# Expert stages: all 40 row gathers issued ahead of the first scatter

## The chip, the core and the metric

One core of a Trainium2 chip runs the whole program. The metric is the device time of one execution in microseconds (us), as the median over runs.

## What is computed

The reference is a stack of six blocks on an input of 8 x 512 tokens of 128 values. The change touches the two "L1" feed-forward blocks (called the expert stages here), of which the reference computes:

```python
logits = xf @ router_w.T
probs = jax.nn.softmax(logits, axis=-1)
topw, topi = jax.lax.top_k(probs, K)                   # K = 2 of E = 8 experts
topw = topw / (topw.sum(-1, keepdims=True) + 1e-06)
order = jnp.lexsort((-fw, fe))                         # by expert, heaviest first
keep = rank < capacity                                 # 1.25 * 4096 / 8 = 640 slots an expert
disp = jnp.zeros((E, capacity + 1, D), x.dtype).at[se, pos].set(xf[st])
g = jnp.einsum('ecd,edf->ecf', disp, wg)
u = jnp.einsum('ecd,edf->ecf', disp, wu)
eo = jnp.einsum('ecf,efd->ecd', jax.nn.silu(g) * u, wd)
contrib = gathered * (sw * keep.astype(x.dtype))[:, None]
out = jnp.zeros_like(xf).at[st].add(contrib)

x = x + 0.5 * _L0_ffn_ref(_layernorm(x, axis=-1), ...)
x = x + _L0_attn_ref(_layernorm(x, axis=-1), ...)
x = x + 0.5 * _L0_ffn_ref(_layernorm(x, axis=-1), ...)
x = x + 0.5 * _L1_ffn_ref(_layernorm(x, axis=-1), ...)  # expert stage s = 0
x = x + _L1_attn_ref(_layernorm(x, axis=-1), ...)
x = x + 0.5 * _L1_ffn_ref(_layernorm(x, axis=-1), ...)  # expert stage s = 1
```

## The kernel before

The program is written out without loops at run time. Each engine has its own instruction stream; they meet at semaphores. The work of most blocks is ordered by a table of due times (`program_order`), but an expert stage stands by itself: the function `experts1(s)` of each engine, for s = 0 (between the second L0 feed-forward block and the L1 attention) and for s = 1 (the end of the program).

An expert stage first searches, for every expert, the weight above which its 640 tokens lie, and writes a table `token_of` of 40 columns: column r = 5 e + t holds the 128 token numbers of tile t of expert e (`SLOT_TILES` = 5, `SLOT_ROWS` = 40). VectorE writes it at L1955. From then on it goes by expert, e = 0 to 7:

- POOL (`gather_rows`, L2066 to L2079) issues one indirect DMA for each column (L2076), which fetches 128 rows of 136 values from the tensor `tokens` in HBM into `rows_in[e]`. Each of the 8 experts has its own `rows_in`: six lie in the memory of a stack buffer, the last two in the arena.
- TensorE turns the gathered tiles (`turn_gathered`, L828), ScalarE and VectorE split them into two halves (L1427, L1969), after which 16 products of three matmuls each follow (L823: eight "gate" and eight "wide" results in five PSUM banks taken in turn). ScalarE applies Silu to a gate result (L1473), VectorE multiplies it with the wide result (L1992). TensorE turns the next expert's tiles and then multiplies with the down weights ("narrow", L1159, 40 matmuls in two parts), and ScalarE scales the result by the slot's weight into `rows_out[e % 2]` (L1486). Before that it waits for the scatters of expert e - 2, which read the same buffer.
- POOL (`scatter_rows`, L2081 to L2091) issues five indirect DMAs (L2088) that add the rows to `sums` (s = 0) or to the output (s = 1) in HBM. Since two experts can write the same token, the first scatter of expert e waits until all of expert e - 1 have landed.
- SyncE loads the weights, 256 KB each (`load`, L2111): gate and up weights of expert e + 3 when those of expert e + 1 have been split, down weights of expert e + 2 when expert e is done.

How far the gathers run ahead is set by two numbers, AHEAD (experts gathered before the first scatter) and BETWEEN (gathers issued ahead of each later expert's scatters), in POOL's `experts1`:

```python
                gathered = AHEAD * SLOT_TILES
                gather_rows(range(gathered))
                for e in range(EXPERTS):
                    if e:
                        more = min(gathered + BETWEEN, SLOT_ROWS)
                        gather_rows(range(gathered, more))
                        gathered = more
                    scatter_rows(e)
```

After stage 0, SyncE waits for the last scatter and loads X back from `sums` (L2111), with which the L1 attention begins. After stage 1 it waits for the last scatter and the program ends.

Of the kernel before, what the change touches and what calls it, by code (L numbers as in the profile page):

```python
# [61 lines left out]
HALF = P // 2  # L62
PER_ROW = P // EXPERTS
REACHED = 4.0
AHEAD, BETWEEN = 4, 4
NARROW = ((0, 2), (2, SLOT_TILES))


# [2245 lines left out]
```

## Time and profile before

| | |
|---|---|
| median of 3 runs | 2848.12 us (2844.03 to 2848.57) |
| profiled execution: its own time | 2866.33 us |
| profiled execution: span | 2864.2 us |
| TensorE busy | 2597.2 us (91%) |
| VectorE busy | 2070.6 us (72%) |
| ScalarE busy | 1913.6 us (67%) |
| POOL busy | 1673.6 us (58%) |
| mean granted TensorE clock | 0.955 |
| indirect DMAs issued by POOL | 80 gathers (L2076), 80 scatters (L2088) |

Busy time is what the engine spent in instructions; for an indirect DMA on POOL that is the time in which POOL makes the DMA's descriptors, not the transfer. The shares are means over the whole program; the expert stages take some 200 us at two places, about 1570 to 1780 us and 2655 to 2864 us. In a timeline the bracket behind an instruction says how long its engine had stood idle before it, and what ended that. "issue" is time in which nothing that the profile shows was waited for.

### The profile page before, as it was taken

How to read it: one execution, taken by the hardware profiler on the slowest of the kernel's cores; microseconds unless marked ns; L12 is line 12 of the kernel's file. 1: busy time of each engine (PE TensorE's matmuls, PEld its weight loads, DVE VectorE, ACT ScalarE, POOL GpSimd, SP SyncE). 2: the span in 40 equal slices, each digit the busy share in tenths (PEclk: the TensorE clock that was granted, in tenths of full speed). 3: DMA queues.
4: the chain of work that ended last, by engine and by line, in shares of the span. 5: the costliest groups of instructions: out<-in, count | busy, mean ns of one | idle time of the engine just before them, and what ended most of it. 6: DMA issues, size and time to landing. Idle time of an engine off the chain costs nothing. (4 is left out here: it accounts for less than half of the span.)

```text
span 2864.2 us, 51642 instructions
## 1 busy us (share of the span) xinstructions
PE 2597.2 (91%) x18932; PEld 1774.7 (62%) x18932; DVE 2070.6 (72%) x4694; ACT 1913.6 (67%) x4049; POOL 1673.6 (58%) x836
## 2 busy tenths in 40 slices
PE   7999999999999999998998286999999999998286
PEld 6996555555555565646887176565665666665176
DVE  5677888888888889885776633778778778776632
ACT  5665777687777777776775143878778778776143
POOL 0002989898989889893110176656556556555077
PEclk9999999999999999998999598999999999999588
DMA  3014554454544454540001244000000000000133
GB/s 107 1 60 111 120 122 120 114 139 112 133 113 120 119 130 113 122 101 16 20 17 27 69 89 67 1 2 9 9 2 9 9 2 9 9 2 9 40 80 51
DMA packets 144649, 179.21 MB, mean 63 GB/s; under 512 B 30547, under 2 KB 74128, under 8 KB 143888
## 3 DMA queue, kind: packets, MB, share of 16 engines
q1 hardware_dynamic: 130320, 165.20, 22.8%
q0 software_dynamic: 14080, 10.73, 2.8%
q8 instruction: 152, 2.49, 0.4%
q14 instruction: 97, 0.79, 0.1%
HBM read 56.51 MB, written 17.72 MB: 26 GB/s over the span
## 5 line engine op out<-in xcount | busy, mean ns | idle before, releaser
L2047 POOL TENSOR_TENSOR arena<-arena 128x2048 f32<-128x2048 f32 x192 | 882.0, 4595 | 216.9 <-ACT arena L1353 200.3
L1658 DVE TENSOR_REDUCE top<-psum 128x1 f32<-128x512 f32 x1024 | 649.4, 683 | 79.5 <-PE psum L937 79.4
L937 PE MATMUL psum<-stack 98*128 98x512 f32 (+1 forms) x2048 | 604.8, 423 | 15.6 <-ACT arena L1353 9.3
L1353 ACT ACTIVATE arena<-psum 128x512 f32<-128x512 f32 x1024 | 546.6, 599 | 48.1 <-PE psum L937 47.7
L1008 PE MATMUL psum<-arena,values 128*32 128x512 f32 (+1 forms) x3072 | 484.5, 603 | 3.5 <-ACT arena L1353 2.6
L937 PEld LDWEIGHTS psum<-stack 98*128 98x128 f32 (+1 forms) x2048 | 357.1, 191 | 210.3 <-DVE top L1658 87.5
L2057 POOL TENSOR_TENSOR by_query<-by_query,row_tables 128x1024 f32<-128x1024 f32 x170 | 321.7, 1900 | 217.1 <-DVE row_tables L1664 215.9
L1656 DVE TENSOR_REDUCE row_tables<-psum 128x1 f32<-128x512 f32 x512 | 335.6, 679 | 2.7 <-PE psum L945 1.7
L1008 PEld LDWEIGHTS psum<-arena,values 128*32 128x32 f32 (+1 forms) x3072 | 128.6, 119 | 276.7 <-issue 252.2
L1676 DVE COPY arena<-psum 128x512 f32<-128x512 f32 x256 | 175.7, 689 | 120.4 <-PE psum L989 119.4
L2017 POOL TENSOR_SCALAR rstd<-mv 128x4 f32<-128x4 f32 x56 | 13.2, 235 | 415.6 <-DVE mv L1522 413.2
L1369 ACT ACTIVATE by_query<-psum,row_tables 128x512 f32<-128x512 f32 x340 | 231.6, 690 | 12.2 <-DVE row_tables L1656 8.9
L2057 POOL TENSOR_TENSOR arena<-arena,row_tables 128x1024 f32<-128x1024 f32 x86 | 162.8, 1899 | 118.9 <-DVE row_tables L1664 118.2
L1401 ACT ACTIVATE arena<-psum 128x512 f32<-128x512 f32 x128 | 76.9, 601 | 205.2 <-PE psum L1008 205.2
L823 PE MATMUL psum<-stack 128*128 128x512 f32 x768 | 212.9, 414 | 0.6 <-DVE X L1612 0.5
L1612 DVE SCALAR_TENSOR_TENSOR X<-psum,weight,X 128x128 f32<-128x128 f32 x512 | 144.0, 344 | 83.9 <-PE psum L889 83.1
L1382 ACT ACTIVATE arena<-psum 128x512 f32<-128x512 f32 x256 | 153.6, 603 | 63.1 <-PE psum L989 61.4
L1273 ACT ACTIVATE arena<-arena 128x512 f32<-128x512 f32 x256 | 158.6, 629 | 54.0 <-DVE arena L1603 44.3
L889 PEld LDWEIGHTS psum<-arena 128*128 128x128 f32 x1536 | 184.9, 192 | 7.0 <-ACT arena L1273 0.4
L889 PE MATMUL psum<-arena 128*128 128x128 f32 x1536 | 186.6, 275 | 0.0
L823 PEld LDWEIGHTS psum<-stack 128*128 128x128 f32 x768 | 138.5, 193 | 24.9 <-DVE X L1612 0.9
L1992 DVE TENSOR_TENSOR arena<-psum,arena 128x320 f32<-128x320 f32 x128 | 60.7, 490 | 128.1 <-ACT arena L1473 64.4
(208 smaller groups left out, 4685.1 us busy)
## 6 DMA issues: line engine op xcount, KB each, us to landing
stack<-halves SPq DMA_DIRECT2D x768, 128.0 KB, 2.4
qk_ring<-qk_split SPq DMA_DIRECT2D x64, 256.0 KB, 2.9
v_ring<-v_split SPq DMA_DIRECT2D x32, 256.0 KB, 3.0
tokens<-xn SPq DMA_DIRECT2D x16, 256.0 KB, 2.4
arena<-in_wg SPq DMA_DIRECT2D x16, 256.0 KB
arena<-in_wu SPq DMA_DIRECT2D x16, 256.0 KB
arena<-in_wd SPq DMA_DIRECT2D x16, 256.0 KB
wqkv<-in_w_qkv SPq DMA_DIRECT2D x2, 1536.0 KB, 9.1
```

What stands on the lines that cost most here:

```text
L823: ins = T_.matmul(out_ap, weights[w], moving[m], start=i == 0, stop=i == 2)
L889: ins = T_.matmul(bk[:, t * P:(t + 1) * P], h[:, c, t * P:(t + 1) * P], w[:, c, :], start=c == 0, stop=c == 1)
L937: return T_.matmul(bk, st[0:k, side, h, cols], st[0:k, 1 - side, h, :], start=True, stop=True)
L1008: ins = T_.matmul(bk[c, :], values[:, n % N_VALUES, kt, c], by_key[n % 2][:, kt, h, :] if l else prob[(n * TILES_B + kt) % N_PROB][:, h, : ...
L1273: S_.activation(part, part, ACT.Square).then_inc(squared, 1)
L1353: S_.activation(prob[tile % N_PROB][:, h, :], psum[:, bank[key], :], ACT.Exp, scale=scale).then_inc(released[bank[key]], 1)
L1369: S_.activation(by_query[i // HEADS[1] % len(by_query)][:, h, :], psum[:, bank[key], :], ACT.Exp, bias=peak[n % 2][:, qt, h:h + 1], accum_ ...
L1656: V_.reduce_max(peak[i][:, qt, h:h + 1], psum[:, bank[key], :], AX.X, negate=True).then_inc(peaked, 1)
L1658: give(V_.reduce_max(top[i][:, j:j + 1], psum[:, bank[key], :], AX.X), key)
L1676: give(V_.tensor_copy(by_key[n % 2][:, :, :, j * HALF:(j + 1) * HALF], psum[:, bank[key], :].rearrange("p (t h q) -> p t h q", t=TILES_B, ...
L2047: G_.tensor_tensor(to, old, prob[tile % N_PROB], ALU.add).then_inc(summed, 1)
L2057: G_.tensor_tensor(rows[:, :, :], rows[:, :, :], row_share[n % 2][:, qt, :].unsqueeze(2).to_broadcast([P, HEADS[1], SEQ]), ALU.mult).then_ ...
```

## The change

AHEAD becomes 8, so that `gathered` is 40 before the loop and `gather_rows` gets an empty range each time within it.

```diff
-AHEAD, BETWEEN = 4, 4
+AHEAD, BETWEEN = 8, 4
```

On POOL, stage 0 (`tokens` gathered to `rows_in` and, for experts 6 and 7, to the arena; `sums<-arena` are the scatters):

```order
 L2076 DMA rows_in_71<-tokens,arena 128x136 x5
 L2076 DMA rows_in_72<-tokens,arena 128x136 x5
-L2088 DMA sums<-arena 4736x128 x5
-L2076 DMA rows_in_73<-tokens,arena 128x136 x4
-L2088 DMA sums<-arena 4736x128 x5
-L2076 DMA rows_in_73<-tokens,arena 128x136
-L2076 DMA rows_in_74<-tokens,arena 128x136 x3
-L2088 DMA sums<-arena 4736x128 x5
-L2076 DMA rows_in_74<-tokens,arena 128x136 x2
-L2076 DMA arena<-tokens,arena 128x136 x2
```

The 20 gathers of experts 4 to 7 stood in groups of four behind the scatters of experts 0 to 4.

```order
+L2076 DMA rows_in_73<-tokens,arena 128x136 x5
+L2076 DMA rows_in_74<-tokens,arena 128x136 x5
+L2076 DMA arena<-tokens,arena 128x136 x10
+L2088 DMA sums<-arena 4736x128 x40
```

Now the 40 gathers stand in one row, and the 40 scatters behind them in another. Stage 1 moves in the same way, with `out<-arena` as its scatters. The instructions of TensorE, VectorE, ScalarE and SyncE, and their order, are the same.

## Rows read from the trace of the kernel before

**Rows 1.** The page: the span, and TensorE's granted clock in 40 slices.

```profile
span 2864.2 us, 51642 instructions
...
PEclk9999999999999999998999598999999999999588
```

**Rows 2.** Stretches of the first expert stage: us, busy by engine, clock, DMA share, GB/s.

```profile
core 0: us, PE busy (x) PEld busy (x) DVE busy (x) ACT busy (x) POOL busy (x), PEclk, DMA share, GB/s
1632.00:1659.00 27.00, 10.79 (x45) 9.07 (x45) 4.88 (x11) 5.28 (x10) 20.37 (x20) 0.67 0.32 88
1659.00:1668.00 9.00, 7.28 (x42) 6.83 (x43) 2.84 (x7) 2.60 (x7) 0.00 (x0) 0.66 0.05 10
1668.00:1743.50 75.50, 72.89 (x527) 68.69 (x525) 34.44 (x74) 37.51 (x98) 61.61 (x45) 1.00 0.46 89
```

**Rows 3.** POOL's timeline, first expert stage: start us, us, instruction [idle before it <-releaser].

```profile
1632.48 1.42 POOL L2076 DMA_INDIRECT rows_in<-tokens,arena  x1 [63.25 <-DVE arena L1955]
...
1657.64 1.00 POOL L2076 DMA_INDIRECT rows_in<-tokens,arena  x1 [0.30 <-issue]
1668.46 1.63 POOL L2088 DMA_INDIRECT sums<-arena  x1 [9.83 <-ACT arena L1486]
...
1683.44 1.62 POOL L2088 DMA_INDIRECT sums<-arena  x1 [0.30 <-issue]
...
1743.79 1.62 POOL L2088 DMA_INDIRECT sums<-arena  x1 [0.30 <-issue]
...
1751.34 1.55 POOL L2088 DMA_INDIRECT sums<-arena  x1 [0.30 <-issue]
1755.35 1.55 POOL L2088 DMA_INDIRECT sums<-arena  x1 [2.46 <-DMA sums<-arena]
...
1766.86 1.97 POOL L2088 DMA_INDIRECT sums<-arena  x1 [2.52 <-DMA sums<-arena]
...
1774.71 1.56 POOL L2088 DMA_INDIRECT sums<-arena  x1 [0.30 <-issue]
```

**Rows 4.** POOL's timeline, second expert stage.

```profile
2740.13 1.00 POOL L2076 DMA_INDIRECT rows_in<-tokens,arena  x1 [0.30 <-issue]
2750.28 1.62 POOL L2088 DMA_INDIRECT out<-arena  x1 [9.16 <-ACT arena L1486]
...
2848.75 1.55 POOL L2088 DMA_INDIRECT out<-arena  x1 [2.54 <-DMA out<-arena]
```

**Rows 5.** TensorE's timeline, first expert stage.

```profile
1643.53 6.84 PE L823 MATMUL psum<-halves,stack 128*128 128x320 f32 x30 [1.40 <-DVE halves L1969]
1651.93 0.70 PE L823 MATMUL psum<-halves,stack 128*128 128x320 f32 x3 [1.56 <-issue]
...
1661.85 1.97 PE L823 MATMUL psum<-halves,stack 128*128 128x320 f32 x6 [1.72 <-DVE arena L1992]
...
1669.28 7.58 PE L823 MATMUL psum<-halves,stack 128*128 128x320 f32 x48
...
1677.54 4.73 PE L1159 MATMUL psum<-arena 128*128 128x128 f32 x40
...
1718.43 4.73 PE L1159 MATMUL psum<-arena 128*128 128x128 f32 x40 [0.46 <-DVE arena L1992]
...
1731.34 4.73 PE L1159 MATMUL psum<-arena 128*128 128x128 f32 x40 [0.30 <-DVE arena L1992]
...
1745.20 0.77 PE L828 MATMUL psum<-cst,arena 128*128 128x128 f32 x5 [1.79 <-DMA arena<-tokens,arena]
...
1758.15 4.73 PE L1159 MATMUL psum<-arena 128*128 128x128 f32 x40 [0.68 <-DVE arena L1992]
```

**Rows 6.** ScalarE's timeline: an expert's output is scaled (L1486).

```profile
1666.94 0.63 ACT L1486 ACTIVATE arena<-psum,arena 128x128 f32<-128x128 f32 x2 [1.47 <-PE psum L1159]
...
1760.32 0.63 ACT L1486 ACTIVATE arena<-psum,arena 128x128 f32<-128x128 f32 x2 [2.75 <-DMA sums<-arena]
```

**Rows 7.** The chain of waits, first expert stage: start us, us, what.

```profile
1656.14 5.07 another core or an unknown queue
```

## The prediction

> **What bounds the kernel now.** I read the page first: span and clock slices [rows 1]. TensorE runs at its higher level (2.4 GHz) nearly everywhere; the low digits lie at the two expert stages, where the change is. Next the windows of the first expert stage [rows 2]: while POOL issues its first 20 gathers TensorE is busy for 10.79 of 27 us, then POOL stands still for 9 us, and from 1668 to 1743.5 us POOL is busy for 61.61 of 75.5 us. Nearly all of the missing 13.9 us are the 0.30 us between one DMA and the next (45 of them), so POOL is full there, at least as long as TensorE.
>
> POOL's timeline [rows 3] gives its prices. The first 20 gathers start at 1632.48 and the last of them at 1657.64; in the steady part one costs 1.00 + 0.30 = 1.30 us. Then POOL is idle for 9.83 us, until ScalarE has the first output. A scatter costs 1.55 + 0.30 to 1.62 + 0.30 us. With four gathers between experts, the turn from the first scatter of expert 0 (1668.46) to that of expert 5 (1743.79) takes 15.07 us an expert. With none between, from expert 5 (1743.79) to 6 (1755.35) it is 11.56 us and from 6 to 7 (1766.86) 11.51: the last scatter's issue at 1751.34 is followed by the next expert's first at 1755.35, after 4.01 us, of which 2.46 us are idle waiting for the landing. The gathers cover that wait now.
>
> TensorE's timeline [rows 5] shows a second thing. At expert 0 it issues 30 matmuls in one row from 1643.53 (10 products, as many as the PSUM banks take at first), and then only groups of three with gaps: five products from 1651.93 to 1661.85, four steps of 2.48 us each. Expert 1 takes 7.58 us for 16 products, 0.47 us each. The chain of waits has a piece of 5.07 us in that stretch that ends on no engine of this core [rows 7]. The gathers' last issue ends at 1658.64, and the crawl ends at about 1661.3, 2.65 us later. I read this as: **while the long row of gathers is in flight, results of TensorE are noticed late**, one per 2.48 us.
>
> **The change, step by step.** It removes no instruction. The 20 gathers of experts 4 to 7 go ahead of the first scatter, past 5 x 5 = 25 scatters at most, on POOL alone; SyncE's queue and the other engines' order stay.
>
> 1. *POOL's own chain.* The 40th gather starts at 1657.64 + 20 x 1.30 = 1683.64, the first scatter can start at 1684.94, where it started at 1668.46. Seven turns of 11.54 us (mean of 11.56 and 11.51) bring the first scatter of expert 7 to 1765.7. Before it was 1766.86 [rows 3]: -1.1 us. POOL gains the 9.83 us of idle time, and pays it back in five more waits of 2.5 us. In stage 1 [rows 4]: 2740.13 + 21 x 1.30 + 7 x 11.54 = 2848.2 against 2848.75: -0.5 us. Sum -1.6 us. With POOL alone, the change is worth nothing.
>
> 2. *TensorE's chain.* If the crawl lasts as long as gathers are in flight, it now ends 2.65 us after 1684.64, at 1687.3. At 1661.3 ten of expert 0's 16 results had been noticed. The other six and the two turned parts of expert 1's tiles (POOL still gathering) take 8 x 2.48 = 19.8 us, to 1681.1; 1.4 us later (ScalarE's and VectorE's halves, as the idle time before 1643.53) expert 1's products can begin, five fill the banks, and the other 11 follow at 0.47 us from 1687.3: 1692.5, with 0.7 us up to the narrow matmuls (from 1669.28 + 7.58 to 1677.54 [rows 5]) 1693.2. Before it was 1677.54: **15.7 us later**. From there the pace is that of rows without a wait for gathers: 1718.43 to 1731.34 is 12.91, and 1731.34 to 1758.15 less the 1.79 us that expert 7's tiles were late, halved, is 12.51. I take 12.7. Six of them: narrow matmuls of expert 7 at 1769.4 (before 1758.15). The first scatter follows by 1760.32 - 1758.15 = 2.17 us to ScalarE [rows 5, 6] and 1668.46 - 1666.94 = 1.52 us to POOL [rows 3, 6]: 1773.1. That is later than POOL's own 1765.7, so it decides: 1773.1 - 1766.86 = +6.2 us, and the five scatters and the landing behind it (issue of the fifth at 1774.71 now) move with it. What is gained against step 1, the 1.79 us wait for expert 7's tiles, is in the pace.
>
> 3. *Stage 1* is built alike, its gathers' last start 2740.13 and its POOL idle 9.16 us [rows 4]. The same lengths from its own end of gathers (2741.13 + 26.0 + 2.65 = 2769.8, then 5.9, 76.2 and 3.7 us) give 2855.6 against 2848.75: +6.8 us.
>
> Small edits at nothing: ScalarE's output of expert 2 waits for the scatters of expert 0 to land, which now is some 1696 us; with TensorE 15 us later that is covered. If TensorE were not late, it would cost 2 to 3 us at expert 2 that POOL's chain hides. HBM traffic stays the same, and the DMA share is 0.46 at most [rows 2].
>
> Sum: **+13 us**. On the profiled execution's own 2866.33 us that is 2879.3; on the median of the runs, 2848.12, it is 2861. The rows hold no 40 gathers in one go, so the crawl's cost is bounded: if it doesn't go on past where it ends now, step 1 decides and the sum is -1.6. If nothing at all of expert 0 gets through until 1687.3, its last products and narrow matmuls start some 8 us behind step 2, and both stages give +29. I take the measured rate, because 13 more us of gathers passed at it.
>
> The Trainium skill ("SBUF — State Buffer", Who interferes with whom) states that a DMA never contends with a compute engine, TensorE among them. By it there would be no crawl to prolong, and the sum would be step 1's. The trace so far speaks against a full reading of it: 2.48 us a product beside gathers, 0.47 without [rows 5].
>
> **Rivals.**
>
> - *The crawl belongs to profiling.* The profiled execution is 18.2 us above the median, and the two idle stretches of POOL are 9.83 + 9.16 = 19.0 us [rows 3, 4], close to it. If in the timed runs expert 0 isn't slowed, POOL has no idle time to give: its first scatter comes at 1658.9 and expert 7's at 1757.3. After the change it is 1765.7. That is 26.0 us of gathers put ahead, less 5 turns that get shorter by 15.07 - 11.54 = 3.53 us: +8.4 us a stage, +17 us in all, 2865. For it: the near-equal numbers. Against it: nothing shows where those 18 us are.
> - *Not slower: the crawl ends by itself.* TensorE isn't held past 1661 (the stretch from 1668 us on has gathers and TensorE at 72.89 of 75.5 us [rows 2]), step 1 decides, and the result is -1.6 us: 2846.5. It decides from the point where expert 7's narrow matmuls start before 1762. The Trainium skill's rule ("DMA: Bandwidth & Descriptors", Rules for kernel authors) to issue a DMA early and wait for it late points this way. The trace has gathers that were late once a stage, by 1.79 us at expert 7 [rows 5], and that wait isn't where the stage ends.
> - *Faster.* The 4.01 us between an expert's last scatter and the next's first shrink, with no gathers sharing the queue, to the plain step of 1.9 us. POOL's turn is then 9.4 us and its chain ends early; TensorE's, at 1758.15 - 1.79 + 3.7 = 1760.1, gives -6.8 us a stage: 2834.5. The two turns without gathers around them in flight (11.56 and 11.51) speak against it.
> - *Worse crawl*, the upper bound above: 2877.
>
> That the change doesn't do what it says is excluded by the order of POOL's instructions.
>
> **Numbers.** 0.2% is 5.7 us, about what a measurement of this kernel can tell from no change. Forecast 0.45, profiling rival 0.25, crawl ends by itself 0.20, faster 0.05, worse crawl 0.05. Slower by over 0.2%: 0.45 + 0.25 + 0.05 = 0.75. Within: 0.20. Faster: 0.05. The predicted time is the likeliest case's, 2861. The range goes from the "not slower" case with room, 2846, to 2870, above the profiling rival and half-way to the worse crawl.
>
> **What would show it.** In the changed profile: the 40th gather at 51 us behind the first, the first scatter right behind it, turns of 11.5 us where POOL decides or 12.7 us where ScalarE's output does (POOL idle until L1486, not until the DMA). TensorE in groups of three up to about 1687, expert 1's narrow matmuls near 1693, expert 7's near 1769. I am wrong on step 2 if TensorE goes through expert 1 at 0.47 us a product while gathers are issued; wrong on the rival if the timed runs and the profile move by the same amount.

## The result, and the profile after

The changed kernel takes 2866.76 us as the median of 4 runs (2865.57 to 2870.71), the kernel before 2848.35 us in the 4 runs beside them (2844.03 to 2853.35). The ratio is 1.0078 with a 95% interval of 1.0066 to 1.0090: **slower by 0.8%**. By the medians that is 18.4 us, by the ratio 22 us (19 to 26), and 2848.12 x 1.0078 is 2870.3, just past the upper end of the range. The two figures do not fully agree: the medians alone have a ratio of 1.0065, just below the interval. The traces further down give 18.3 us.

The changed kernel's profiled execution took 2865.57 us, the fastest of its four. Its page, against [rows 1]:

```profile
span 2863.5 us, 51642 instructions
...
PEclk9998999999999999999999598999999999999588
```

The span is 0.7 us *shorter* than in the profile before (2864.2). So the two profiles show no loss at all, and the timed runs show 18 us. One of the two traces isn't like the timed runs, and it is the one of before, on which the prediction rests: its own time of 2866.33 us lies 18 us above its median. That has to be kept in mind in each comparison below.

POOL's timeline of the first expert stage, against [rows 3] (start us, us, instruction, [idle before it <-releaser]):

```profile
1629.99 1.42 POOL L2076 DMA_INDIRECT rows_in<-tokens,arena  x1 [63.20 <-DVE arena L1955]
...
1681.69 1.00 POOL L2076 DMA_INDIRECT arena<-tokens,arena  x1 [0.30 <-issue]
1682.99 1.63 POOL L2088 DMA_INDIRECT sums<-arena  x1 [0.30 <-issue]
...
1690.55 1.56 POOL L2088 DMA_INDIRECT sums<-arena  x1 [0.30 <-issue]
1694.65 1.56 POOL L2088 DMA_INDIRECT sums<-arena  x1 [2.54 <-DMA sums<-arena]
...
1764.30 1.89 POOL L2088 DMA_INDIRECT sums<-arena  x1 [2.38 <-DMA sums<-arena]
...
1772.08 1.57 POOL L2088 DMA_INDIRECT sums<-arena  x1 [0.30 <-issue]
```

The second stage, against [rows 4]:

```profile
2766.17 1.00 POOL L2076 DMA_INDIRECT arena<-tokens,arena  x1 [0.30 <-issue]
2767.47 1.63 POOL L2088 DMA_INDIRECT out<-arena  x1 [0.30 <-issue]
...
2848.01 1.55 POOL L2088 DMA_INDIRECT out<-arena  x1 [2.59 <-DMA out<-arena]
```

The 40 gathers end 53.0 us after the first one starts, the first scatter follows without idle time (9.83 us before), and now each expert's scatters wait 2.4 to 2.5 us for the landing of those before: a turn from 1682.99 to 1764.30 is 81.31 / 7 = 11.62 us. From the first gather to the first scatter of expert 7 it is 134.31 us, in the profile before 134.38. In stage 1 it is 133.34 and was 133.84.

TensorE's timeline, against [rows 5]:

```profile
1640.97 9.20 PE L823 MATMUL psum<-halves,stack 128*128 128x320 f32 x48 [1.40 <-DVE halves L1969]
...
1650.84 4.73 PE L1159 MATMUL psum<-arena 128*128 128x128 f32 x40
...
1663.59 4.73 PE L1159 MATMUL psum<-arena 128*128 128x128 f32 x40
...
1680.81 2.01 PE L823 MATMUL psum<-halves,stack 128*128 128x320 f32 x12
1695.37 7.52 PE L823 MATMUL psum<-halves,stack 128*128 128x320 f32 x36 [12.55 <-ACT arena L1486]
...
1754.29 4.73 PE L1159 MATMUL psum<-arena 128*128 128x128 f32 x40 [0.68 <-DVE arena L1992]
```

No crawl: expert 0's 48 matmuls stand in one row of 9.20 us, in the middle of the gathers (the granted clock was 0.64 from 1638 to 1648 us and 1.00 after it; expert 1's 48 matmuls then take 7.59 us, also beside gathers). Expert 1's narrow matmuls come 33.6 us after the first gather, where the prediction had 60.7 (1693.2 - 1632.48). At expert 3 TensorE now stands for 12.55 us. ScalarE's rows for the output scaling (L1486), against [rows 6], tell why:

```profile
1652.99 0.63 ACT L1486 ACTIVATE arena<-psum,arena 128x128 f32<-128x128 f32 x2 [1.59 <-PE psum L1159]
...
1693.92 1.40 ACT L1486 ACTIVATE arena<-psum,arena 128x128 f32<-128x128 f32 x5 [17.03 <-DMA sums<-arena]
...
1756.46 0.63 ACT L1486 ACTIVATE arena<-psum,arena 128x128 f32<-128x128 f32 x2 [2.75 <-PE psum L1159]
```

Expert 2's scaling waits 17.03 us until expert 0's scatters, which start so much later, have landed and free the output buffer. It holds up ScalarE's Silus for expert 3, and with them TensorE. All the same, expert 7's output is there at 1756.46, and POOL comes to it only at 1764.30.

For the five-microsecond piece of the chain [rows 7] there is no counterpart in this profile. The idle time of POOL before scatters (L2088), summed over the program (us, times), by what ended it:

```profile
its engine sat idle before it (us, times) until:
...
  DMA sums<-arena: 17.3, 7
  DMA out<-arena: 16.9, 7
  ACT arena L1486: 0.3, 1
```

34.2 us in 14 waits for the landing. The profile before had 10.0 us in four, and 19.9 us for ScalarE's output.

### The profile page after: what moved, and what is told of

Its sections match the earlier page's. It is cut to its first block and busy times, and to the rows that moved or that the text cites. A ratio compares the mean times of both kernels' runs of the same rounds, so it can differ in the third digit from the quotient of the medians.

```text
span 2863.5 us, 51642 instructions
## 1 busy us (share of the span) xinstructions
PE 2593.0 (91%) x18932; PEld 1775.6 (62%) x18932; DVE 2070.8 (72%) x4694; ACT 1913.9 (67%) x4049; POOL 1668.9 (58%) x836
## 5 line engine op out<-in xcount | busy, mean ns | idle before, releaser
L1992 DVE TENSOR_TENSOR arena<-psum,arena 128x320 f32<-128x320 f32 x128 | 60.8, 489 | 129.5 <-ACT arena L1473 121.3
L823 PE MATMUL psum<-halves,stack 128*128 128x320 f32 x768 | 128.3, 327 | 27.7 <-ACT arena L1486 24.5
```

The source lines that it names most:

```text
L823: ins = T_.matmul(out_ap, weights[w], moving[m], start=i == 0, stop=i == 2)
```

## The experiments

Each was timed beside the kernel before, and differs from it, or from the change where the text says so, by what its diff shows.

### Was the profile before like the timed runs?

The kernel before, unchanged and profiled anew.

> The kernel before, unchanged, profiled a second time. If TensorE's crawl at expert 0 (products 2.48 us apart beside the gathers) belonged to that one execution or to chance, the new profile shows 16 products in some 9 us and POOL without the 9.8 us of idle time, and the profiled execution's own time lies near the timed runs, about 2848 us. If the crawl comes with every profile of this order of gathers, it is there again and the profiled time is near 2866 us while the timed runs stay near 2848. Ratio 1.000 either way.

Measured: median 2847.22 us, ratio 0.9998 (0.9989 to 1.0007). The profiled execution took 2854.55 us: not the 2848 expected, but the slowest of its eleven. POOL and TensorE in the new profile (span 2852.4 us):

```profile
1639.47 1.43 POOL L2076 DMA_INDIRECT rows_in<-tokens,arena  x1 [63.26 <-DVE arena L1955]
...
1664.64 1.00 POOL L2076 DMA_INDIRECT rows_in<-tokens,arena  x1 [0.30 <-issue]
1665.94 1.63 POOL L2088 DMA_INDIRECT sums<-arena  x1 [0.30 <-issue]
...
1740.49 1.62 POOL L2088 DMA_INDIRECT sums<-arena  x1 [0.30 <-issue]
...
1748.03 1.55 POOL L2088 DMA_INDIRECT sums<-arena  x1 [0.30 <-issue]
1752.09 1.55 POOL L2088 DMA_INDIRECT sums<-arena  x1 [2.51 <-DMA sums<-arena]
...
1763.66 2.02 POOL L2088 DMA_INDIRECT sums<-arena  x1 [2.58 <-DMA sums<-arena]
...
1772.11 1.56 POOL L2088 DMA_INDIRECT sums<-arena  x1 [0.30 <-issue]
```

```profile
1650.46 9.85 PE L823 MATMUL psum<-halves,stack 128*128 128x320 f32 x48 [1.40 <-DVE halves L1969]
...
1660.98 4.73 PE L1159 MATMUL psum<-arena 128*128 128x128 f32 x40
...
1741.83 1.33 PE L828 MATMUL psum<-cst,arena 128*128 128x128 f32 x5 [3.57 <-DMA arena<-tokens,arena]
...
1756.20 4.73 PE L1159 MATMUL psum<-arena 128*128 128x128 f32 x40 [0.67 <-DVE arena L1992]
```

The crawl isn't there. Expert 0's matmuls take 9.85 us, the first scatter starts at 26.47 us after the first gather, straight behind the 20th gather, and not at 35.98. Expert 7's first scatter comes at 124.19 us instead of 134.38, the last scatter of all at 132.64. **In an execution without the crawl, POOL has no idle time between gathers and scatters in the kernel before.** The crawl was in that one execution. Of ten profiles of this study (the two here, the change and seven variants) only the first has it: in the nine others expert 0's 48 matmuls take 9.15 to 9.85 us in both stages. And of the 48 timed executions of the kernel before, none took more than 2854.55 us. What made the crawl isn't known; nothing tried here brought it back.

The new profile isn't free of a disturbance either: it is 7 us above its median. That part lies ahead of the expert stages (the first gather starts at 1639.47 us, in the changed kernel's profile at 1629.99). So the spans of the two differ by 11 us only, and lengths are compared from here on within a stage, from its first gather.

Against this profile the change's cost is in the trace: first gather to last scatter 142.09 us against 132.64 in stage 0, and 140.79 against 131.90 in stage 1 (read in the same way from both traces). That is +9.4 and +8.9, together 18.3 us, as much as the difference of the medians (18.4). POOL's waits in this profile are:

```profile
its engine sat idle before it (us, times) until:
...
  DMA out<-arena: 5.9, 2
  DMA sums<-arena: 5.1, 2
```

11.0 us in four waits (two bare gaps in each stage), against 34.2 us in 14. The ten added waits hold 23.2 us. That isn't all loss: each takes the place of the usual 0.30 us between two DMAs (3 us), and each saves a switch between kinds (after one, a gather takes 1.09 us and the next 1.05 instead of 1.00, a scatter 1.62 instead of 1.55: some 0.2 us a gap, 2 us). 18 us are left.

### Bare waits or a late first scatter?

Two things went together in the change: the scatters begin 26 us later, and five more gaps between experts are left bare. Two kernels with 30 gathers ahead part them, one with two gathers in each of five gaps, one with 4, 4 and 2.

```diff
-AHEAD, BETWEEN = 4, 4
+AHEAD, BETWEEN = 6, 2
```

> 30 gathers ahead, then two in each of five gaps. Theory of the uncovered waits: a gap with two gathers (2.6 us) covers the 2.5 us that POOL waits for the landing of the scatters before, so only the last two of seven gaps are bare, as before: +0 to +2 us on 2848. Theory of the late first scatter (what counts is how much later the scatters begin, 13 us a stage): half of the change's cost, +9 us or more.

Measured: 2848.17 us, ratio 1.0003 (0.9994 to 1.0013): +1 us (-2 to +4).

```diff
-AHEAD, BETWEEN = 4, 4
+AHEAD, BETWEEN = 6, 4
```

> 30 gathers ahead, then 4, 4 and 2. Theory of the uncovered waits: four of seven gaps are bare instead of two, at some 1.85 us each and twice in the program: +7 us. Late first scatter: the same as with two gathers a gap, +9 us. The difference to the kernel with two a gap is the test: +5 to +7 us by the first, 0 by the second.

Measured: 2859.93 us, ratio 1.0045 (1.0031 to 1.0059), which is +12.8 us (9 to 17).

Both begin their scatters 40 us after the first gather in stage 0 (40.2 and 39.7), 13 us later than before. One costs nothing, the other 13 us. So a late first scatter costs nothing by itself, and what counts is whether the gaps are covered. A gap with two gathers:

```profile
1678.03 1.55 POOL L2088 DMA_INDIRECT sums<-arena  x1 [0.30 <-issue]
1679.89 1.09 POOL L2076 DMA_INDIRECT arena<-tokens,arena  x1 [0.31 <-issue]
...
1682.63 1.62 POOL L2088 DMA_INDIRECT sums<-arena  x1 [0.30 <-issue]
```

From the last scatter of one expert to the first of the next it is 4.60 us, and POOL waits for nothing but its issue. Two gathers take up what the landing takes, and of their 2.6 us they cost only some 0.6 there (a turn mostly takes 12.1 to 12.6 us, a bare one 11.5 to 11.8). That is why this kernel is as fast as the one before: in stage 0 its first scatter starts 13.7 us later, and its seven turns are together 13.3 us shorter. The size for the second kernel was missed: +7 expected from 1.85 us a gap, +12.8 timed; its trace has 3.6 us more than before from first gather to last scatter in stage 0 (136.2 against 132.6) and 5.0 in stage 1 (136.9 against 131.9). These 8.6 us lie nearer to the expectation, and just below the timed interval; what the rest is isn't shown.

A finer step between: 35 ahead, one gather in each of five gaps.

```diff
-AHEAD, BETWEEN = 4, 4
+AHEAD, BETWEEN = 7, 1
```

> 35 gathers ahead, then one in each of five gaps. Theory of the bare waits: a gather of 1.3 us hides wholly in a wait of 2.5 us, so the turn stays at 11.6 to 11.8 us and each stage is 5 x 1.3 = 6.5 us shorter than with 40 ahead: the change less some 12 us, +6 to +8 us on before. Late first scatter (20 more gathers cost 18.4 us, so 15 more cost three quarters): +14 us.

Measured: 2856.32 us, ratio 1.0032 (1.0019 to 1.0044): +9.1 us (5 to 13). The turns of stage 0 stayed at 11.5 to 12.1 us (11.4 to 12.0 in the change), so one gather hides almost wholly. The interval leaves out the +14 of the late first scatter, if narrowly.

### Is the wait free time for POOL?

Two small instructions whose result nobody uses, before each expert's scatters but the first, in the change and in the kernel before:

```diff
+        scratch = carve(32, 4)
...
                 def scatter_rows(e):
+                    if e:
+                        for k in range(2):
+                            G_.tensor_tensor(scratch[:, (s * EXPERTS + e) * 2 + k, :], ones[:, 0:4], minus_half[:, :], ALU.pow)
```

> The change, with two small POOL instructions of some 1.05 us each put into each of the seven gaps between two experts' scatters (work that nobody uses). Theory of the bare waits: POOL waits 2.4 to 2.6 us in each of the seven gaps, so 2.2 us of work hide there: +0 to +2 us on the change, +18 to +24 on before. If POOL's time there were not a wait: 7 x 2.2 x 2 = +31 us on the change.

> The kernel before with the same filler. Five of its seven gaps are already full with four gathers, so the filler is paid there: 5 x 2.2 x 2 = +22 us; in the two bare gaps it costs nothing. If the gathers weren't what covers the wait: +0 as in the changed kernel, or +31.

Measured: in the change 2865.17 us, ratio 1.0062 (1.0049 to 1.0076), which is +17.7 us on before, as without filler. In the kernel before 2864.98 us, ratio 1.0059 (1.0045 to 1.0073), +16.8 us (13 to 21). The same 28 instructions are free in one kernel; in the other the 20 of them that stand in filled gaps cost their whole time. In the change, one gap:

```profile
1690.19 1.56 POOL L2092 DMA_INDIRECT sums<-arena  x1 [0.30 <-issue]
1691.21 2.61 POOL L2085 TENSOR_TENSOR arena<-ones,minus_half 128x4 f32<-128x4 f32 x2
1694.24 1.60 POOL L2092 DMA_INDIRECT sums<-arena  x1 [0.42 <-issue]
```

From the last scatter of an expert to the next one's first it is 4.05 us with 2.61 us of work in it; without it was 4.10 (1690.55 to 1694.65). In the kernel before, a filled gap and one of the two bare ones:

```profile
1671.89 1.55 POOL L2092 DMA_INDIRECT sums<-arena  x1 [0.30 <-issue]
1673.75 1.09 POOL L2077 DMA_INDIRECT rows_in<-tokens,arena  x1 [0.30 <-issue]
...
1677.80 1.00 POOL L2077 DMA_INDIRECT rows_in<-tokens,arena  x1 [0.30 <-issue]
1678.82 2.24 POOL L2085 TENSOR_TENSOR arena<-ones,minus_half 128x4 f32<-128x4 f32 x2
1681.25 1.65 POOL L2092 DMA_INDIRECT sums<-arena  x1 [0.19 <-issue]
...
1755.77 1.54 POOL L2092 DMA_INDIRECT sums<-arena  x1 [0.30 <-issue]
1756.77 2.60 POOL L2085 TENSOR_TENSOR arena<-ones,minus_half 128x4 f32<-128x4 f32 x2
1759.81 1.60 POOL L2092 DMA_INDIRECT sums<-arena  x1 [0.43 <-issue]
```

In the first the filler of 2.24 us stands behind four gathers, and the gap is 9.36 us. In the second, without gathers, the same filler is free: 4.04 us. So within one kernel the gap decides what the work costs. The kernel's filled turns take 16.6 to 17.2 us, and from the first gather to the last scatter it is 141.1 us in both stages: 8.5 + 9.2 = 17.7 us more than before. That agrees with the timed 16.8 and is below the 22 expected, because the filler takes 2.04 to 2.24 us and 0.1 to 0.2 us of the usual 0.30 falls away behind it.

### ScalarE's wait for the output buffer

The most visible new wait of the changed kernel is the 17.03 us of ScalarE and TensorE's 12.55 us behind it. A third output buffer takes most of it away:

```diff
-        rows_out = [carve(SLOT_TILES, DIM) for _ in range(2)]
+        rows_out = [carve(SLOT_TILES, DIM) for _ in range(3)]
...
-                    if e >= 2:
-                        act.wait_ge(*all_scattered(s, e - 2))
+                    if e >= 3:
+                        act.wait_ge(*all_scattered(s, e - 3))
...
-                            ins = S_.activation(rows_out[i][:, t, :], psum[:, bank[key], (t - lo) * P:(t - lo + 1) * P],
+                            ins = S_.activation(rows_out[e % 3][:, t, :], psum[:, bank[key], (t - lo) * P:(t - lo + 1) * P],
...
-                            rows_out[e % 2][:, t, :], None, bounds_check=(TILES if s else SLOT_TILES + TILES) * P - 1,
+                            rows_out[e % 3][:, t, :], None, bounds_check=(TILES if s else SLOT_TILES + TILES) * P - 1,
```

> The change (all 40 ahead) with three output buffers instead of two, so that ScalarE waits for the scatters of expert e - 3 and not e - 2. POOL's chain decides: the same as the change, +18 to +20 us on before, and TensorE's 12.5 us of waiting at expert 3 get shorter without any gain. If ScalarE's wait for the output buffer were the cause: back by up to 12 us a stage, near 2848.

Measured: 2871.91 us, ratio 1.0087 (1.0073 to 1.0101), +25 us (21 to 29): no gain on the change, and somewhat above the 18 to 20 expected (its trace has 20.3 us more than before from first gather to last scatter, in both stages together). TensorE's last narrow matmuls of stage 0:

```profile
1743.27 4.73 PE L1159 MATMUL psum<-arena 128*128 128x128 f32 x40 [0.68 <-DVE arena L1992]
```

ScalarE's longest wait for the buffer in stage 0 is now 4.62 us, and TensorE starts these matmuls 110.9 us after the first gather (1632.42), 13 us earlier than in the change (124.3); and yet expert 7's first scatter still comes at 136.2 us. With the 3.7 us from those matmuls to POOL, TensorE has some 21 us in hand there. The new wait on the busiest engine was only where its slack went.

### Fewer gathers ahead

```diff
-AHEAD, BETWEEN = 4, 4
+AHEAD, BETWEEN = 3, 5
```

> 15 gathers ahead, then five in each of five gaps. POOL reaches the first scatter at 19.9 us after the first gather, but expert 0's output is there only at some 24.6 us (in the changed kernel's trace TensorE starts those matmuls 20.9 us after the first gather, and 3.7 us follow to POOL): POOL idles 4.7 us a stage, and covered and bare waits are as before: +9 to +10 us. If an earlier first scatter were worth something in itself: faster than before.

Measured: 2855.16 us, ratio 1.0033 (1.0022 to 1.0044): +9.4 us (6 to 13).

```profile
1648.80 1.00 POOL L2076 DMA_INDIRECT rows_in<-tokens,arena  x1 [0.30 <-issue]
1654.66 1.63 POOL L2088 DMA_INDIRECT sums<-arena  x1 [4.86 <-ACT arena L1486]
```

POOL runs out of gathers and stands for 4.86 us until expert 0's output. 20 gathers ahead is just what covers this first wait, and at least two in each gap covers the others. The last two gaps can't be covered by moving gathers: TensorE turns expert e + 1's tiles ahead of expert e's narrow matmuls, so expert 7's gathers must be issued before expert 6's scatters, and put into the gap just ahead of those they would hold up expert 6's output (this follows from the order of the instructions and wasn't tried). No version here beats the kernel before; the one with 6 and 2 equals it.

## Why the prediction was wrong

- **Step 1, POOL's own chain: right in its durations, set against the wrong base.** 40th gather plus 1.30 at 52.5 us after the first, measured 53.0. Turns of 11.54, measured 11.62. First scatter of expert 7 sooner by 1.1 and 0.5 us than in the profile before; measured 0.07 and 0.50. But the sentence drawn from it, "POOL gains the 9.83 us of idle time", fails: an ordinary execution has no such idle time (26.47 us to the first scatter instead of 35.98), so nothing stands against the ten added waits. The turns and the start were sized well; the idle time to be gained was not there.
- **Step 2, TensorE's chain: the step that failed.** "While the long row of gathers is in flight, results of TensorE are noticed late" was a reading of one execution. With twice as many gathers in a row, TensorE does expert 0 in 9.20 us; expert 7's narrow matmuls came 124.3 us after the first gather and not 136.9, and POOL decides. The +6.2 and +6.8 us of this step were never there. That their sum, +13, is of the sign and near the size measured is chance.
- **The profiling rival: right in its arithmetic and in its base, half right in its cause.** It took POOL without idle time and summed 26.0 us of gathers, less five turns shorter by 3.53 us, to +8.4 a stage; the traces give +9.4 and +8.9. In stage 0 the first scatter starts 26.5 us later and not 26.0, and up to expert 7's the turns give back 16.4 us and not 17.65: the turn with four gathers is 14.91 us in the new profile of before ((1740.49 - 1665.94) / 5) and not 15.07, and a bare one 11.62 and not 11.54. Its reason wasn't right: the crawl doesn't belong to profiling, since nine other profiled executions have none. It was one disturbed execution. I had the clue, 18.2 us above the median against 19.0 us of POOL's idle time, and gave it 0.25; the main sum should have been made from it.
- **"Small edits at nothing": too small.** ScalarE's wait for expert 0's scatters was put at 2 to 3 us if TensorE isn't late. It was 17.03 us, since ScalarE and TensorE run ahead of POOL when not held up. That POOL's chain hides it was right, as the third buffer shows.
- **A reading of the rows that was too smooth.** "Four steps of 2.48 us each" is a mean: in the trace the five starts lie 2.07 to 2.90 us apart.
- **The other rivals** fell: "not slower" had step 1's base, "faster" needed the 4.01 us between two experts to shrink, and they stayed, and "worse crawl" needed a crawl. The Trainium skill's rule to issue a DMA early and wait for it late ("DMA: Bandwidth & Descriptors", Rules for kernel authors) brought no gain here: issued earlier, 20 gathers a stage cost 18 us in all, as issuing itself is what fills POOL. With the Trainium skill's rule that a DMA never contends with a compute engine ("SBUF — State Buffer", Who interferes with whom) the trace agrees: expert 1's 48 matmuls take 7.59 us beside gathers and expert 5's 7.58 without. I had read the crawl as speaking against it.

## What to carry to other kernels

When the profiled execution lies above the median by about as much as an idle stretch that the argument uses, take a second profile (and look where that one's own surplus lies) or make the sum without that stretch. On a queue whose engine is the bound, independent work costs nothing only where it stands in a wait between dependent operations; collected in front it leaves those waits bare, so spread it, as much per gap as the wait is long (here two gathers of 1.3 us for 2.5 us). A long new wait on the busiest engine says nothing until it is known which chain ends last.

## What the runs showed that was not expected

One execution had TensorE's results come late at two places, both at expert 0 of a stage, with groups of matmuls starting 2.1 to 2.9 us apart instead of 0.47, and nothing to give it away but 0.6% more time (mean granted clock 0.955, in the new profile of the same kernel 0.952). VectorE's products (L1992) in that first profile:

```profile
1655.65 0.49 DVE L1992 TENSOR_TENSOR arena<-psum,arena 128x320 f32<-128x320 f32 x1 [3.77 <-remote]
1661.30 1.40 DVE L1992 TENSOR_TENSOR arena<-psum,arena 128x320 f32<-128x320 f32 x3 [5.16 <-remote]
```

Their waits end on no engine that the profile can name ("remote"), and at 1661.30 three products follow without a pause, as from a backlog. That fits results that were ready and noticed late, but doesn't prove it. The cause stays open.

The next expert's first scatter mostly starts 4.0 to 4.1 us after the start of the last one, of which 1.56 us are its issue and 2.4 to 2.6 us are waited, in the bare gaps of the change as in those of the kernel before (single gaps: 3.5 to 4.9 us). The Trainium skill ("DMA: Bandwidth & Descriptors", Anatomy of one DMA) puts the fixed cost of a DMA from this queue at about 2.0 us, most of it the receipt of the write; the wait in the trace, 2.4 to 2.6 us, is of that size and somewhat longer. One rival had it shrink without gathers in the queue; it didn't.
